# Four-layer graph network on one core: a shared buffer for the two accumulating ranges, 8 slots of gathered rows for 6, and tail sums added in pairs

## The reference

```python
x = ln(x + tanh(segment_sum(sigmoid([x[src], rel[type]] @ att) * x[dst], src) @ W0.T + b0))   # round 0
x = ln(x + where(deg > 0, segment_sum(x[src], dst), x) @ W1.T + b1)                           # gather layer l = 0
x = ln(x + segment_sum(x[src] * w[:, None], dst))                                             # gather layer l = 1
x = ln(x + segment_sum(x[src] * (w * w2)[:, None], dst))                                      # gather layer l = 2
```

## Time and profile before

| | |
|---|---|
| median of 3 runs | 11979.11 us (11966.0 to 11984.94) |
| the profiled execution | 11878.79 us, its span 11877.0 us |
| mean granted TensorE clock | 0.806 |
| PE, DVE, ACT, POOL busy | 8897.3, 7726.7, 5860.3, 8022.3 us |
| gather layer 0 (first gather to last tail matmul) | 3946.8 to 6484.2 us |
| gather layer 1 | 6572.1 to 9177.5 us |
| gather layer 2 | 9228.4 to 11825.9 us |

### The profile page before, as it was taken

How to read it: one execution, slowest core, us unless ns; L and a number is a source line. 1 busy time by engine, 2 the same in 40 slices (tenths; PEclk the granted TensorE clock), 3 DMA queues, 4 the chain that set the end, 5 groups by cost and what they waited for, 6 DMA issues and landing times. The chain is left out here.

```text
span 11877.0 us, 171360 instructions
## 1 busy us (share of the span) xinstructions
PE 8897.3 (75%) x49605; PEld 5666.5 (48%) x49606; DVE 7726.7 (65%) x19171; ACT 5860.3 (49%) x13187; POOL 8022.3 (68%) x7169
## 2 busy tenths in 40 slices
PE   4787888888886455566666787888887788888887
PEld 2444444444444234444546455454445455554445
DVE  8777777777774655544444776666665776666665
ACT  4766555555553444333332665544443766544443
POOL 5787788888887566666665566666665566666665
PEclk8877777777776676767777899989988899889998
DMA  5433333334334211111111111111111111111111
GB/s 145 47 38 35 36 37 38 39 38 38 38 38 70 51 25 25 25 25 24 24 24 27 27 24 25 25 25 24 25 24 28 28 25 25 25 25 25 23 24 30
DMA packets 651932, 398.90 MB, mean 34 GB/s; under 512 B 456994, under 2 KB 563748, under 8 KB 649745
## 3 DMA queue, kind: packets, MB, share of 16 engines
q0 software_dynamic: 445920, 252.47, 17.5%
q1 hardware_dynamic: 201276, 132.08, 4.3%
q10 hardware_dynamic: 3814, 3.37, 0.1%
HBM read 283.23 MB, written 104.16 MB: 33 GB/s over the span
## 5 line engine op out<-in xcount | busy, mean ns | idle before, releaser
L801 POOL DMA_INDIRECT mem<-xt,mem x5175 | 4910.8, 949 | 2864.1 <-issue 1338.3
L1148 PE MATMUL ps<-mem 128*128 128x392 f32 (+5 forms) x6750 | 2905.2, 536 | 1079.8 <-DVE mem L1708 448.9
L722 POOL DMA_INDIRECT table<-mem,idx x1925 | 3000.4, 1559 | 746.4 <-issue 556.7
L1708 DVE TENSOR_TENSOR mem<-mem,ps 128x392 f32 (+3 forms) x3300 | 1917.4, 581 | 1966.8 <-remote 1007.5
L943 ACT ACTIVATE mem<-iota_f,mem 128x128 f32<-128x128 f32 x4200 | 1319.3, 390 | 2659.8 <-remote 1312.7
L1160 PE MATMUL ps<-mem,xs 128*64 128x94 f32 (+1 forms) x17640 | 2068.5, 271 | 382.5 <-issue 363.2
L1160 PEld LDWEIGHTS ps<-mem,xs 128*64 128x64 f32 (+1 forms) x17640 | 1803.8, 156 | 1026.7 <-issue 979.8
L1689 DVE TENSOR_SCALAR mem<-ps,mem 128x392 f32<-128x392 int16 (+5 forms) x4050 | 2175.9, 556 | 0.0
L1148 PEld LDWEIGHTS ps<-mem 128*128 128x128 f32 (+1 forms) x6750 | 1106.1, 184 | 1936.5 <-issue 1312.5
L922 ACT COPY mem<-zero_c 128x658 f32<-128x658 f32 x1260 | 895.6, 732 | 1370.5 <-remote 896.1
L1181 PE MATMUL ps<-mem 128*64 128x64 f32 (+1 forms) x10350 | 1031.7, 245 | 478.4 <-issue 456.2
(11 more groups left out here) (180 smaller groups left out, 7819.2 us busy)
## 6 DMA issues: line engine op xcount, KB each, us to landing
mem<-xt,mem POOLq DMA_INDIRECT x5175
mem<-key_rows SPq DMA_DIRECT2D x385, 160.0 KB
table<-mem,idx POOLq DMA_INDIRECT x1925
table<-mem POOLq DMA_DIRECT2D x3, 6304.0 KB
mem<-table SPq DMA_DIRECT2D x42, 448.0 KB, 5.2
xt<-xs SPq DMA_DIRECT2D x9, 896.0 KB
mem<-in_x_dram SPq DMA_DIRECT2D x415, 16.0 KB
w_d<-mem SPq DMA_DIRECT2D x2, 1562.5 KB, 7.8
```

The source lines that it names most:

```text
L722: pool.indirect_dma_start(out=tables[i % NTAB][:, :], out_offset=bass.IndirectOffsetOnAxis(ap=idx[:, i % (IDXS * GC):i % (IDXS * GC) + 1], ...
L801: pool.indirect_dma_start(out=gbuf[:, o:o + F], out_offset=None, in_=xt[l][:, :], in_offset=bass.IndirectOffsetOnAxis(ap=src_q[q % 2].bitc ...
L1148: last = pe.matmul(ps_d[b % PSD][:, 0:w], lo_l[:, r * P:(r + 1) * P], blk_l[:, r * DT:r * DT + w], start=(k == 0), stop=(k == parts - 1))
L1708: v.tensor_tensor(at, at, new, ALU.add).then_inc(d_add[l], 1)
```

## The change

1. Tail sums: `ps_w` has four buffers (two to a PSUM bank). DVE does `tail_add` for two slots at once, in every odd slot n, for the slots n - 3 and n - 2. PE's tail matmuls wait for those adds only in even slots. One-hots of the tail are made one slot ahead (n + 1) and not two; there are four buffers for them, not three.
2. `R` = 8 slots of gathered rows.
3. One table of 188 columns takes the place of two of 94. A segment uses a window of 126 of its columns: even segments the first 126 upwards, odd ones the last 126 with the direction reversed. 64 columns in the middle are shared. A segment starts in the part that is its own, and at block `SHARED_AT` DVE waits until the segment before is flushed and cleared. There are 22 flushes a layer of 126 columns, and a flush is planned into the stretch before that block.
4. The lists of keys and weights are loaded in smaller pieces (100 and 23 for 170 and 45), which makes the room in SBUF.

```diff
-R = 6
-OHR = 3
+R = 8
+OHR = 4
+SHARED_AT = [next((b for b in range(a, z) if block_row(b) - block_row(a) > EX - D - 4), z) if s_ else a
+             for s_, (a, z) in enumerate(zip(SEGS, SEGS[1:]))]
...
-        zones = [(max(len(blocks) // 5, 2) + z * len(blocks) * 7 // (10 * FZ), z) for z in range(FZ if s_ else 0)]
+        alone = SHARED_AT[s_] - SEGS[s_] if s_ < NSEG else 0
+        start = max(alone // 8, 2)
+        zones = [(start + z * max(alone * 7 // 8 - 4 - start, 0) // FZ, z) for z in range(FZ if s_ else 0)]
...
-QD, QT = 170, 45
+QD, QT = 100, 23
...
                         if s_:
                             pe.wait_ge(f_add[l], s_)
+                            pe.wait_ge(cleared[l], s_ * FZ)
...
-                    if n >= 2:
-                        pe.wait_ge(acc_add[l], n - 1)
+                    if n >= 4 and n % 2 == 0:
+                        pe.wait_ge(acc_add[l], n - 2)
...
-                    if b == SEGS[s_] and s_ >= 2:
-                        v.wait_ge(cleared[l], (s_ - 1) * FZ)
+                    if s_ and b == SHARED_AT[s_]:
+                        v.wait_ge(cleared[l], s_ * FZ)
...
-                    v.wait_ge(agg_done[l], n + 1)
-                    v.tensor_tensor(at, at, ps_w[n % 2][0:M, :], ALU.add).then_inc(acc_add[l], 1)
+                    v.wait_ge(agg_done[l], min(n // 2 * 2 + 2, NT))
+                    v.tensor_tensor(at, at, ps_w[n % 4][0:M, :], ALU.add).then_inc(acc_add[l], 1)
...
                 for n in range(NT):
-                    if n:
-                        tail_add(n - 1, ZONE_END[n - 1] // FZ)
-                    if n + 2 < NT:
-                        tail_hots(n + 2)
+                    if n >= 3 and n % 2:
+                        for m in (n - 3, n - 2):
+                            tail_add(m, flushed)
+                        added = n - 1
+                    if n + 1 < NT:
+                        tail_hots(n + 1)
```

More of the change, by code:

```diff
@@ L157, in trailing_slots @@
     assert blocks[-1] == NBLK and zones[-1] == NSEG * FZ
-    for s_ in range(2, NSEG):
-        freed = next(n for n in range(NT) if zones[n + 1] >= (s_ - 1) * FZ)
-        assert freed < next(n for n in range(NT) if blocks[n + 1] > SEGS[s_])
+    for s_ in range(1, NSEG):
+        freed = next(n for n in range(NT) if zones[n + 1] >= s_ * FZ)
+        assert SHARED_AT[s_] == SEGS[s_ + 1] or freed < next(n for n in range(NT) if blocks[n + 1] > SHARED_AT[s_])
     return blocks, zones
@@ L365, in program @@
         nkt = key_f[:, 0:C0]
-        DENSE_AT = 9730
-        dense = [mem[:, DENSE_AT + p * WC * T:DENSE_AT + (p + 1) * WC * T] for p in range(2)]
-        LISTS_AT = DENSE_AT + 2 * WC * T
+        DENSE_AT = 10700
+        LISTS_AT = DENSE_AT + RW * T
+        dense = mem[:, DENSE_AT:LISTS_AT].rearrange("p (s d) -> p s d", s=T)
+        window = [dense[:, :, p * EX:p * EX + WF] for p in range(2)]
         kd_q, nslo_q, wd_q, src_q, dst_q, wt_q = ([mem[:, at + p * n:at + (p + 1) * n] for p in range(2)] for n, at in (
@@ L1180, in _ @@
                         q = (n % OHR) * OW + k * WD
-                        last = pe.matmul(ps_w[n % 2][0:M, :], gbuf[:, o:o + M], ohr[:, q:q + WD], start=(k == 0),
+                        last = pe.matmul(ps_w[n % 4][0:M, :], gbuf[:, o:o + M], ohr[:, q:q + WD], start=(k == 0),
                                          stop=(k == GC - 1), skip_group_check=True)
@@ L1290, in _, with within_window @@
             spread_bases(bmin[:, 0:NB0], segb0, sbase0, SEGS0)
+            def within_window(blocks_n):
+                for a, h, z in zip(SEGS, SHARED_AT, SEGS[1:]):
+                    for lo, hi, most in ((a, min(h, blocks_n), EX - D), (h, min(z, blocks_n), WF - D)):
+                        if lo < hi:
+                            ins = v.tensor_scalar(boff[:, lo:hi], boff[:, lo:hi], 0.0, float(most), ALU.max, ALU.min)
+                link(ins)
             link(v.tensor_tensor(boff, bmin, segb, ALU.subtract))
-            link(v.tensor_scalar(boff, boff, 0.0, float(WC - D), ALU.max, ALU.min))
+            within_window(NBLK)
             link(v.tensor_tensor(bmin, boff, segb, ALU.add))
@@ L1303, in _ @@
             v.tensor_copy(brow[:, CD:C].rearrange("o (g k) -> o g k", k=GC), bc(gmin, NT, GC)).then_inc(base_done, 1)
+            for s_ in range(1, NSEG, 2):
+                for rows in sorted(set(ROWS_OF[SEGS[s_]:SEGS[s_ + 1]])):
+                    lo, hi = (f(b for b in range(SEGS[s_], SEGS[s_ + 1]) if ROWS_OF[b] == rows) for f in (min, max))
+                    ins = v.tensor_scalar(boff[:, lo:hi + 1], boff[:, lo:hi + 1], -1.0, float(RW - rows), ALU.mult, ALU.add)
+            link(ins)
             v.tensor_copy(offs_i[:, 0:NBLK], boff)
@@ L1751, in _ @@
                         hot = hots_up_to(hot, b + 1)
-                for s_ in range(ZONE_END[NT - 1] // FZ, NSEG):
-                    flush_add(s_, NT - 1)
-                tail_add(NT - 1, NSEG)
+                for s_ in range(flushed, NSEG):
+                    flush_add(s_, added)
+                for n in range(added, NT):
+                    tail_add(n, NSEG)
                 v.wait_ge(acc_add[l], NT)
```

70 lines of the change are left out of this document (38 added, 32 removed).

## The result

The changed kernel took 12016.16 us in the median of 7 runs (12000.75 to 12024.66), the kernel before 11975.67 on the same chip (11966.0 to 11984.94, 7 runs). The ratio is 1.0036, 95% interval 1.0026 to 1.0045. Forecast were 11846 us, 1.1% faster; the time lies inside the range of 11640 to 12060, on the side to which the text gave 0.25.

The account below looks back on a forecast made before the run. POOL's gathers, with pauses for PE's late-seen counts, were taken to set the pace. Terms -128 - 50 + 25 + 20 = -133 us took the profiled 11878.8 to 11746; adding 100.3 for the median gave 11846 us, range 11640 to 12060.

Parts of the forecast that it names:

- tail sums in pairs, -178 us: DVE's stop for the tail sum in every slot would vanish nearly whole, winning 128 and 50 us.
- The 128 us: Gather layers 1 and 2: their excess over layer 0, 68 + 60 us, counted as won by pairing tail sums.
- The 50 us: POOL's pauses: counts arriving in twos more often would save 0.16 us a slot, a third of 165 us taken.
- Depth, +25 us: Eight slots of rows: POOL issues two slots more at a layer's start, costing 8 us a layer, no steady gain.
- The zone's price: PE's flush matmuls: a zone widened to 126 columns takes 1.69 us instead of 1.29.
- PE's saved 63 us: Fewer, wider flushes: 63 us less PE time in three layers, inside the 128 and not counted again.
- The +20 for packed flushes: Slots with three or more zones go from 8 to 40 and overrun the pace: +20 us, at most 86 if unabsorbed.
- The higher clock: TensorE's granted clock would speed up layer 0's packed flushes; the sum stays, as PE doesn't set that layer's pace.
- The new wait on `cleared`: DVE waits at each segment's first shared block until the last zone is cleared: costed at nothing, two slots' cover.
- Nothing moves: Rival: gathers and pauses set the pace in all layers, DVE's stop moves to the blocks; 11955 to 12003 us, chance 0.17.
- The slower rival: PE falls behind in packed flushes, POOL can't make up: +86 + 37 = +123 us, 12102 us, chance 0.23.
- POOL runs through: Rival: the chain's idle time (449) and PE's flush time (63) both go, -512 us, 11467 us, chance 0.13.

Follow-up runs that it names:

- shared_alone: Kernel before with only the shared table and 22 flushes a layer, six slots of rows, against the kernel before at 11889 us: ratio 1.0008.
- pairs_alone: Kernel before with only the tail sums added in pairs, against the kernel before at 11889 us: ratio 1.0051.
- before_third: The kernel before, unchanged, run again for its profile in the fourth series: 11889 us.
- ramp8: Changed kernel with POOL's look-ahead growing from three slots to eight over a layer's first 40 slots, against the kernel before at 11886 us: ratio 1.0017.
- four_gathers: Kernel before with four of the five gathers in each slot, the fifth tail chunk left out, against the kernel before at 11886 us: 0.8900, 10,576 us.
- r6_t0_s1: Kernel before with only the shared table and 22 flushes a layer, in the series where the kernel before took 10668 us: ratio 1.0020.
- depth_alone: Kernel before with only eight slots of gathered rows for six, against the kernel before at 11889 us: ratio 1.0021.

## Why the prediction was wrong

**The step that failed: tail sums in pairs, -178 us.** It was the only gain in the sum. Measured alone the part costs +61, beside the shared buffer, as in the change, -4 and +7, and this is about all of the gap between the forecast change (-133 us) and the measured one (+43). The two halves of the term fail for different reasons.

The 128 us were the excess of layers 1 and 2 over layer 0, taken as won because PE's waits for DVE's adds (449 us) would shrink. They do shrink by pairs, each time by 40 to 81 us: 440 to 385 alone, 460 to 379 at eight slots, 773 to 733 and 791 to 742 beside the shared buffer. The time follows in none of these. What was wrong is the price of such a wait: in `shared_alone`, without pairs, they are 333 us longer at a cost of 10. Nearly all of them lie beside POOL's pauses and not on the path. (The growth from 449 to 742 us in the changed kernel, and from 11 to 87 before its zones, is the shared buffer's: 773 and 61 in `shared_alone`.) The prediction saw that DVE's idle time moves to the block's sum and called it a gain, because an add and one or two one-hots are done meanwhile. That a DVE which stands at that wait when the late count arrives is no sooner there than one that stood at another is argued and not measured; it fits the 787 us that became 794.

The 50 us were for counts that come in twos. They came in twos no more often: POOL paused for over 0.6 us 789 times in `pairs_alone` for 795 in `before_third`, past a layer's first 15 slots 209 times after two slots on end for 210, and the sum was 1548 us for 1495. (The changed kernel's 724 pauses are again the shared buffer's: 714 in `shared_alone`.) Nor was the wait for the flush add in the working: that the add came "a slot later" was read off the diff for the tail sums alone.

**Depth, +25 us: right.** 0.0021 to 0.0024 is 25 to 29 us, and 37 beside the other parts. The mechanism holds as well: POOL issues two slots more, 12.5 us, and the sums are 11 to 14 us later at slot 30. `ramp8`, which throttles the start, takes about half of the loss back and still ends its layers 10.4 to 12.3 us after the last gather, where the prediction had put a gain of uncertain size. That "no steady gain" follows from POOL, PE and DVE going in step is borne out on the slow kind by four slots being no slower than six. It doesn't hold on the fast kind, where four slots lose 0.4% against eight.

**Flushes.** The zone's price was right (1.65 us for 1.69), and so was leaving PE's saved 63 us out: PE's busy time falls by 107 us in the whole span and the part alone is no faster. The +20 for packed flushes stands against +10 alone, inside its bounds and no clearer than nothing. Of the waits inside it the late last add is real (28 waits, 87 us of PE's idle time before zones, the longest 7.5 us); as the part alone costs 10 us with 61 us of it, most of it must be hidden. The higher clock that the text thought of for layer 0 didn't come: it was granted 0.68 for 0.72, with PE busy 57% of the layer for 59%.

**The new wait on `cleared`** was costed at nothing, and DVE's idle time before line 1738 lists no clear of ACT among its causes. In the changed kernel's trace the last clear ends at least 6.2 us before the first shared add starts, in all 60 cases. Right.

**The picture.** POOL's gathers and pauses set the pace of all layers (`four_gathers`): right, and it should have made the term for pairs small. The argument that forecast -128 contradicted it: PE waits most for adds in layer 0, which is the fastest, so less of this waiting is not what makes a layer fast. Why layers 1 and 2 are longer than layer 0 stays open.

**The rivals.** "Nothing moves" (0.17, 11955 to 12003) had the right reasoning for pairs and shared, and with depth's 25 us its upper end comes within 13 us of what was measured. The slower rival (0.23, 12102) had the right sign and named PE's late waits for DVE's last adds, but its price of 86 for packed flushes is far above the +10 measured (11 to either side), and most of the loss was depth's. "POOL runs through" is what the fast kind does, before any change.

**What stays open.** Why counts are seen late while POOL issues gathers in four of the five series and not in the other: the gathers' durations and gaps are the same in both, and no run here touches the cause, nor tells whether it belongs to a chip or to a time. Depth alone was not measured on the fast kind, and why shared alone costs 0.2% there is not shown: PE's idle time before blocks is 534 us there and 203 with pairs alone, of which 402 and 111 are waits for DVE's block adds.

**A better version.** On the slow kind the kernel before with four slots is 0.11% faster than with six, at the edge of what can be told; the change at six slots equals before. On the fast kind the change with four slots loses 0.7%; the kernel before with four slots, and the change with six, were not run there. No version here was shown to beat the kernel before on both.

## What to carry to other kernels

Find the engine that sets the pace in every stage, and count as a gain only what shortens its own idle time: removing a wait elsewhere moves it to the next wait, here 787 us out of one group and 794 into the next, and 333 us more of PE's waits cost 10. A deeper buffer had a price here at every stage: a longer run before the first feedback puts the consumer behind, and that lag is left over behind the last transfer. It paid only where the counts came in time (with four slots the change loses 0.4% there against eight). Look for the add or flag that a batched wait delays along with the one it is for, and measure on more than one chip, and at more than one time, before a design is tuned to one set of delays.

## What was unexpected in the hardware

The same program took 10668 and 11974 us in two series, 11% apart, at gathers of 950 ns in both. Outside the gather layers both kinds take 4144 us (`before_third`, `r6_t0_s1`); inside them the difference is the time in which POOL waits for counts of PE, 1495 us on one kind and 74 on the other, each pause taking the place of a gap of 0.30 us. The step from the end of a tail sum to DVE's add took 4.2 us on the one and 0.24 us on the other; both sums ended while POOL was issuing. The prediction read from three rows that a pause grows with POOL's run. In `before_third`, of the pauses whose sum had ended before POOL stopped, those after one slot last 1.5 us in the mean and those after two slots 2.4 (some 430 and 140 of them), the one after seven slots at the start of layer 1 lasts 5.72; after nine slots it was 7.27 (`depth_alone`). TensorE's granted clock was higher on the fast kind in layers 1 and 2 (0.97 for 0.90), where PE was busy 88% of the time for 82%.
